# Unit 0's row maxima as own + relu(other - own) over three engines, and V's and Wo's products placed among the score products

## The reference

```python
def lora_linear(x, W, b, Bm, Am):
    out = jnp.einsum('bld,od->blo', x, W) + b
    upd = jnp.einsum('blr,or->blo', jnp.einsum('bld,rd->blr', x, Bm), Am)
    return out + SCALING * upd
x = _layernorm(x)                             # (1, 1024, 256)
q, k, v = (_split(lora_linear(x, W, b, B, A)) for q, k, v)   # 16 heads of 16
scores = jnp.einsum('bhqd,bhkd->bhqk', q, k) * SCALE
out = jnp.einsum('bhqk,bhkd->bhqd', jax.nn.softmax(scores, axis=-1), v)
x = x + lora_linear(out, Wo, bo, Bo, Ao)      # heads joined again
```

## Time and profile before

| | us |
|---|---|
| median of 3 runs | 350.2 (345.63 to 353.56) |
| profiled execution | 349.53 |
| its span, first to last instruction | 347.7 |
| busy: PE, DVE, ACT, POOL | 322.9, 280.4, 241.9, 128.5 |
| PE's mean granted clock | 0.97 of 2.4 GHz |

### The profile page before, as it was taken

The page is one execution under the profiler, slowest core; times in us unless marked ns, Lnnn a source line. Parts: engine busy times, 40 slices in busy tenths (PEclk is TensorE's granted clock), DMA queues, the critical chain, the costliest instruction groups (busy, mean ns, idle before and its releaser), DMA issues.

```text
span 347.7 us, 5546 instructions
## 1 busy us (share of the span) xinstructions
PE 322.9 (93%) x1919; PEld 141.8 (41%) x1919; DVE 280.4 (81%) x471; ACT 241.9 (70%) x465; POOL 128.5 (37%) x133
## 2 busy tenths in 40 slices
PE   7999789999999999999999899999998789699796
PEld 3753343222222222222222244359545645447695
DVE  6466998999999999999999345338689987988774
ACT  1576112888888898989888867994779323668694
POOL 5032018999300000000023001301699949994030
PEclk9999998999999999999999999999999969879899
DMA  7936855354132000000000000000000000000011
GB/s 216 326 51 129 144 166 86 63 117 84 21 78 45 3 0 3 0 3 0 0 3 1 3 1 2 0 2 0 1 2 0 1 0 2 0 2 0 1 62 60
DMA packets 14879, 14.57 MB, mean 42 GB/s; under 512 B 5060, under 2 KB 13191, under 8 KB 14663
## 3 DMA queue, kind: packets, MB, share of 16 engines
q1 hardware_dynamic: 12422, 12.09, 15.4%
q10 hardware_dynamic: 2176, 1.64, 1.6%
q0 software_dynamic: 256, 0.52, 0.9%
HBM read 5.78 MB, written 1.05 MB: 20 GB/s over the span
## 4 chain that ended last, share of the span: by engine, by line
PE 69%; DVE 14%; ACT 8%; POOL 5%; issue 3%; ACTq 0%; DVEq 0%; POOLq 0%
PE ps L1450 17%; PE ps L1436 13%; DVE mx L1126 9%; PE ps L1412 7%; PE ps L1582 6%; PE ps L1594 6%; PE ps L1363 4%; POOL pbuf L777 3%; PE ps L1567 3%; PE ps L1393 2%; PE ps L1626 2%; ACT ps L958 1%; PE ps L1352 1%; PE ps L1331 1%; ACT parts L898 1%
## 5 line engine op out<-in xcount | busy, mean ns | idle before, releaser
L1126 DVE TENSOR_REDUCE mx<-ps 128x1 f32<-128x1024 f32 x128 | 150.3, 1219 | 5.1 <-PE ps L1412 4.0
L913 ACT ACTIVATE pbuf<-ps 128x512 f32<-128x512 f32 x256 | 134.2, 604 | 24.6 <-PE ps L1436 23.6
L1436 PE MATMUL ps<-pack 64*128 64x512 f16 x256 | 75.9, 382 | 3.0 <-ACT pbuf L913 1.9
L1450 PE MATMUL ps<-pbuf,v_slot 128*32 128x512 f32 x512 | 68.0, 604 | 1.3 <-ACT parts L898 1.3
L1412 PE MATMUL ps<-pack 64*128 64x512 f16 x256 | 62.2, 388 | 4.5 <-DVE mx L1126 4.3
L1436 PEld LDWEIGHTS ps<-pack 64*128 64x128 f16 x256 | 18.8, 93 | 76.8 <-ACT pbuf L913 53.4
L777 POOL TENSOR_TENSOR pbuf<-wT 128x1024 f32<-128x1024 f32 (+3 forms) x32 | 48.2, 1533 | 4.7 <-ACT wT L987 4.7
L732 POOL COPY v_slot<-v_sb 128x512 f32<-128x512 f32 x8 | 4.8, 612 | 108.9 <-PE ps L1450 87.4
L708 POOL TENSOR_TENSOR rstd<-rstd,minus_half 128x2 f32<-128x2 f32 x16 | 11.4, 713 | 71.3 <-DVE rstd L1043 71.3
L1220 DVE SCALAR_TENSOR_TENSOR pack<-ps,g_unit,pack 128x512 f16<-128x512 f32 (+1 forms) x40 | 24.7, 640 | 14.5 <-ACT pack L970 14.5
L1582 PE MATMUL ps<-v_sb,w_nat 128*128 128x512 f16 (+1 forms) x160 | 32.7, 351 | 1.8 <-DVE v_sb L1212 1.8
(11 more groups left out here) (143 smaller groups left out, 370.4 us busy)
## 6 DMA issues: line engine op xcount, KB each, us to landing
w_nat<-in_L_ffn_w_dram SPq DMA_DIRECT2D x2, 1024.0 KB, 7.4
pack<-pbuf SPq DMA_DIRECT2D x24, 64.0 KB, 3.1
pack<-pack SPq DMA_DIRECT2D x3, 512.0 KB, 4.3
x_res<-in_L_attn_a_x_dram SPq DMA_DIRECT2D x4, 256.0 KB, 3.8
pack<-parts SPq DMA_DIRECT2D x16, 64.0 KB, 2.4
pack<-parts SPq DMA_DIRECT2D x32, 32.0 KB, 2.0
out_dram<-x_res SPq DMA_DIRECT2D x4, 256.0 KB, 2.1
w_nat<-in_L_attn_b_Wqkv_dram ACTq DMA_DIRECT2D x1, 768.0 KB, 6.3
```

Source lines behind the costliest of these rows:

```text
L913: act.activation(pbuf[:, c % 2, j, :], ps[:, b, :], ACT.Exp, scale=scale_reg).then_inc(drained[b], 1)
L1126: dve.tensor_reduce(mx[:, par, k:k + 1], ps[:, b:b + 2, :].rearrange("p b k -> p (b k)"), AX_X, ALU.max) \
L1436: pe.matmul(ps[:, b, :], k_group[rows, at, j, P * c:P * c + P].rearrange("p g t -> p (g t)"), q_rows[rows, at, qh, j, :].rearrange("p g t ...
L1450: ins = pe.matmul(ps[32 * j:32 * j + 32, PV_BANK, :], v_slot[:, qh, c, j, :], pbuf[:, c % 2, j, :], start=(c == 0), stop=(c == TT - 1))
```

## The change

Unit 0's maximum tiles are formed as own + relu(other - own), where "own" is the half of the keys that stands in the rows which the score matmul of that head reads. POOL multiplies the other rows of unit 0's queries by -1 (turn). PE's first matmul then goes over all 128 rows and gives own - other in the second bank; its second, over the own 64 rows, gives own in the first. ACT writes relu(other - own) to SBUF (take_over_own), and DVE adds that to own and takes the maximum in one instruction with an accumulator. All other units keep the plain maximum.

V is made in two parts: heads 0 to 3 for the eight token tiles in the maximum pass and the lead, heads 4 to 15 as entries of the score ring, one ahead of scores 4, 8, .. 24 of unit 0 and of 4 and 8 of unit 1. Wo's merge is such an entry too, ahead of score 12 of unit 1. V's own weight merge moves behind projections 4 and 5. ACT issues the first shift's transfer itself; later ones stay on SP, in other places of its queue. The Wqkv load goes to SP behind group 3. The thresholds are computed behind the lead's maxima. ACT's loop is unrolled, and ring places come from the planner instead of formulas. PE waits for a group's packing at the first maximum that reads it. Float16 terms and scratch space swap places in SBUF.

```diff
+V_PARTS = ((0, G), (G, H - G))
-KEEP_UP = 2
+KEEP_UP = 5
+BESIDE_FIRST_UNIT = [[] for _ in range(FILLS)]
+BESIDE_FIRST_UNIT[1] = [("proj", 6)]
+BESIDE_FIRST_UNIT[3] = [("proj", 7)]
+for _t, _k in enumerate(range(5, FILLS, 2)):
+    BESIDE_FIRST_UNIT[_k] = [("v", 0, _t)]
+BESIDE_LEAD = [[], [("shift", 0), ("wsum",)], [("v", 0, TT - 2)], [("v", 0, TT - 1)]]
+BESIDE_SCORES = {
+    **{(0, 4 * n + 4): ("v", 1, n) for n in range(TT - 2)},
+    (1, 4): ("v", 1, TT - 2), (1, 8): ("v", 1, TT - 1), (1, 12): ("wt", O_),
+}
...
+            def turn(rows, g, qh, first, last):
+                at = q_rows[rows, g, qh, :, :].rearrange("p j t -> p (j t)")[:, first:last]
+                pool.tensor_scalar(at, at, -1.0, 0.0, ALU.mult, ALU.add).then_inc(turned, 1)
...
+            for j in range(G):
+                pool.wait_ge(head_packed_by_pool[j], 32)
+                other = 1 - score_rows(j)
+                turn(slice(ROWS * other, ROWS * other + ROWS), 0, 0, HALF * j, HALF * j + HALF)
...
+            def take_over_own(u, k):
+                b = PAIR_BANKS[k % 2]
+                act.wait_ge(filled[b], base[b] + u * (FILLS // 2) + (k // 2 + 1))
+                act.activation(over_own[:, k % 2, :], ps[:, b + 1, :], ACT.Relu, scale=-1.0).then_inc(over_own_ready, 1)
...
+            for k in range(FILLS):
+                take_over_own(0, k)
+                if k == 3:
+                    evacuate_weight(V_)
+                for key in BESIDE_FIRST_UNIT[k]:
+                    beside(key)
...
+                if k == 1:
+                    land_shift(act, 0, 0, 0)
...
             def take_max(u, k, par):
                 b = PAIR_BANKS[k % 2]
+                if is_signed(u, k):
+                    dve.wait_ge(over_own_ready, FILLS * u + k + 1)
+                    slot = over_own[:, k % 2, :]
+                    dve.tensor_tensor_reduce(slot, ps[:, b, :], slot, scale=1.0, scalar=LOWEST, op0=ALU.add, op1=ALU.max,
+                                             accum_out=mx[:, par, k:k + 1]).then_inc(drained[b], 1)
+                    return
...
+                if is_signed(u, k):
+                    own = slice(ROWS * score_rows(j), ROWS * score_rows(j) + ROWS)
+                    pe.matmul(ps[:, b + 1, :], q_rows[:, g, qh, j, at], k_group[:, g, j, keys], start=True, stop=True)
+                    pe.matmul(ps[:, b, :], q_rows[own, g, qh, j, at], k_group[own, g, j, keys], start=True, stop=True) \
+                        .then_inc(filled[b], 1)
+                    return
```

More of the change, by code:

```diff
@@ L64 @@
 SHIFT_UNIT = 2.0 ** 15
+LOWEST = -3e38
+V_PARTS = ((0, G), (G, H - G))
 HALF_EXPONENT = 0x3F800000
@@ L112, in setup_order, with ring_keys, is_signed @@
     yield ("proj", 3)
-    yield ("wt", V_)
     yield ("proj", 4)
     yield ("proj", 5)
+    yield ("wt", V_)
 def beside_max_pass():
-    return [("proj", 6), ("proj", 7), *(("v", t) for t in range(TT)), ("wsum",), ("shift",), ("wt", O_)]
+    return [key for behind in (*BESIDE_FIRST_UNIT, *BESIDE_LEAD) for key in behind]
 SPLIT_BEHIND = {2: 6, 5: 7}
+BESIDE_FIRST_UNIT = [[] for _ in range(FILLS)]
[8 more added lines that the diff above has]
+}
+def ring_keys(u):
+    for s in range(STEPS):
+        if (u, s) in BESIDE_SCORES:
+            yield BESIDE_SCORES[u, s]
+        if s == SHIFT_AT and u < NU - 1:
+            yield ("shift", u + 1)
+        yield ("score", u, s)
+def is_signed(u, k):
+    return isinstance(u, int) and u == 0
 QUADS = H // 4
@@ L252, in numbered @@
     return of
-def ring_place(s, last):
-    return s + (s >= SHIFT_AT and not last)
-def ring_fills(place, i):
-    return (place - i) // len(SCORE_BANKS) + 1
 class Banks:
@@ L284, in plan_banks @@
         banks.count[b] += NU * FILLS // 2
-    for i, b in enumerate(SCORE_BANKS):
-        banks.count[b] += (NU - 1) * RING_USES + ring_fills(STEPS - 1, i)
+    ring = itertools.cycle(SCORE_BANKS)
+    for u in range(NU):
+        for key in ring_keys(u):
+            banks.claim(key, next(ring))
     banks.count[PV_BANK] += NU
@@ L566, in group_count, with land_shift @@
             return 16 * 3 * G * (1 if g < NG // 2 else TWO)
+        def land_shift(eng, g, qh, u):
+            is_drained(eng, ("shift", u))
+            n = G * TT // 2
+            for r in (0, 1):
+                rows = SHIFT_ROWS[g // 2]
+                rows = slice(ROWS * r + rows.start, ROWS * r + rows.stop, rows.step)
+                eng.dma_start(q_rows[rows, g, qh, 2 * r:2 * r + 2, :].rearrange("o h t -> o (h t)"),
+                              m_rows[n * r:n * r + n, :]).then_inc(shift_landed, 16)
         def part_is_cut(eng, m, c, s):
@@ L747, in _ @@
                     pool.wait_ge(tern_ready, 4 * n + c + 1)
+            for t in range(TT):
+                is_drained(pool, ("v", 1, t))
             for g in range(NG - 1):
@@ L1142, in _ @@
             cut_max(0, 0)
+            for k in range(LEAD):
+                take_max(1, k, 1)
             src = is_filled(dve, ("wsum",))
@@ L1365, in project @@
                 ins.then_inc(fill_sem(key), 1)
-            def add_bias(out, which):
-                at, n = BIAS_AT[which], 512 if which == "qk" else D
-                pe.matmul(out, onesb[0:NPART, 0:P], bias_rows[:, at:at + n], start=True, stop=False)
             def project_v(key):
-                t = key[1]
-                if t == 0:
+                _, part, t = key
+                first, n = V_PARTS[part]
+                cols = slice(HD * first, HD * first + HD * n)
+                if part == 0 and t == 0:
                     is_drained(pe, ("wt", V_))
@@ L1434, in score_tile @@
-                at = bass.ds(g, 1)
+                key = ("score", u, s)
                 rows = slice(ROWS * score_rows(j), ROWS * score_rows(j) + ROWS)
-                pe.matmul(ps[:, b, :], k_group[rows, at, j, P * c:P * c + P].rearrange("p g t -> p (g t)"),
-                          q_rows[rows, at, qh, j, :].rearrange("p g t -> p (g t)"), start=True, stop=True) \
-                    .then_inc(filled[b], 1)
+                pe.matmul(to_fill(pe, key), k_group[rows, g, j, P * c:P * c + P], q_rows[rows, g, qh, j, :], start=True,
+                          stop=True).then_inc(fill_sem(key), 1)
@@ L1452, in times_v, with beside @@
                 ins.then_inc(pv_chunk if c < TT - 1 else filled[PV_BANK], 1)
-            side = [key for key in beside_max_pass() if key[0] in ("proj", "v")]
+            def beside(key):
+                if key[0] == "shift":
+                    pe.wait_ge(consts, 6)
+                    shift_rows(key[1])
+                else:
+                    setup[key[0]](key)
             for k in range(FILLS):
@@ L1459, in _ @@
                     pe.wait_ge(head_packed_by_pool[k // 4], 32)
+                    pe.wait_ge(turned, k // 4 + 1)
                 max_tile(0, 0, 0, k)
-                if k % 3 != 2 and side:
-                    key = side.pop(0)
-                    setup[key[0]](key)
-            assert not side
+                for key in BESIDE_FIRST_UNIT[k]:
+                    beside(key)
             pe.wait_ge(second_half_packed, 16 * G)
```

204 lines of the change are left out of this document (83 added, 121 removed).

## The result

| | before | after |
|---|---|---|
| median, us | 351.3 (4 executions, 345.63 to 353.56) | 357.8 (4 executions, 357.33 to 358.33) |
| ratio | | 1.0285, 95% interval 1.0166 to 1.0404 |
| profiled execution | 349.53 | 357.33 |
| its span | 347.7 | 355.5 |
| busy: PE, DVE, ACT, POOL | 322.9, 280.4, 241.9, 128.5 | 330.3, 273.4, 253.2, 131.2 |

The changed kernel is slower by 2.9% (1.7 to 4.0); this ratio, like those of the experiments, leaves out executions more than 1.5% above the fastest of the same kernel, and the two medians alone lie 1.9% apart. The forecast was 1.5%, so the sign was right and the size too small; 357.8 lies just above the forecast's own range of 352 to 357.5. In the two traces the span grows by 7.8 us, where the sum had 5.2.

A forecast was written before the change was run, and what follows sets the result against it. DVE's maxima bound unit 0's pass and the units, where PE's slack is small too. 349.5 - 2.1 (A) - 1.2 (B) + 6.5 (C) + 2.0 (D) = 354.7 us; own range 352 to 357.5, with rivals 346.0 to 359.5.

The forecast's parts named there:

- the sum: Whole kernel: 349.5 - 2.1 - 1.2 + 6.5 + 2.0 = 354.7 us, 1.5% above the kernel before.
- A, the maximum pass: Unit 0's pass: maxima formed with relu replace 16 plain ones; the cut ends at 50.75 against 52.85, -2.1 us.
- The rings: Unit 0's pass: two tiles in flight through PE, ACT and DVE take 0.71 + 0.60 + 0.81 + 0.13 = 2.25 us.
- only exchanged with two projections: Unit 0's pass: despite the new place of V's merge, PE starts tile 0 at 29.25 as before.
- was almost free: V of heads 4 to 15 cost almost nothing where it lay before, since DVE was the slower engine there.
- B, the lead: Between unit 0's cut and the units: cut to end of tile 6 takes 8.5 instead of 9.7, -1.2 us.
- C, V among the scores: Units 0 and 1: eight V entries at 0.9 each, +7.2 us, less about 0.7 once: +6.5; bounds 0 and +11.
- the credit of 0.7 for a finished tile: Units: about 0.7 us saved once, as DVE finds a finished tile waiting when PE falls behind.
- D, Wo's merge: Unit 1: the merge as an entry costs 2.1 plus 0.1 less ACT's 0.2, +2.0 us; bounds 0 and 2.3.
- The units did not swallow the work: First rival: V and Wo's merge cost nothing in the units, under DVE's maxima; 346.2 us, chance 0.17.
- The paired instruction doesn't run at half rate: Second rival: in unit 0's pass DVE's paired sum and maximum takes 1.18 + 0.12 instead of 0.81; 357.8 us, chance 0.16.
- The third, PE's clock: Third rival: PE at its lower clock for 3 to 4 us around the lead costs up to 2; 356.7 us, chance 0.10.

The follow-up runs named there:

- e1: The changed kernel with unit 0's sixteen maxima plain again, without sign change or relu; V and Wo's merge stay in the units: 357.24 us.
- e2: The changed kernel with all of V beside the maximum pass again, Wo's merge in the lead, thresholds ahead of the lead's maxima: 351.61 us, ratio 1.0102.
- e10: The kernel before, with only the first shift's transfer issued by ACT behind its copy instead of by SP: 351.04 us, ratio 1.0012.
- e4: The changed kernel without the lead's five padding matmuls (KEEP_UP = 0): 353.02 us.
- e5: The changed kernel with three padding matmuls behind the cut's transposes instead of five ahead of the lead's first score: 355.01 us.
- e9: The changed kernel with three padding matmuls behind the cut's transposes instead of the lead's five, and V in two halves of eight heads: 351.55 us, ratio 1.0236.
- e6: The changed kernel with each entry, V's and Wo's, two scores later and the same work: 361.51 us.
- e12: e9 with Wo's merge back in the lead, behind the last V, and out of unit 1: 351.09 us, ratio 1.0145.
- e3: The changed kernel without V's two products in the eight entries for heads 4 to 15; bias product, ring place and copy stay: 350.64 us.
- e7: The changed kernel with V in two halves of eight heads, so entries have 128 columns instead of 192: 353.62 us.

## Why the prediction was right in sign and too small

**A, the maximum pass: better than the sum, and in the main for another reason.** The parts were close: 0.70 for DVE instead of 0.81, 0.60 for ACT. The rings came to 2.13 to 2.21 and not 2.25. What sets them is open: two signed tiles and V take PE 2.13 as worked out, and with 0.70 in place of 0.81 the sum's chain of three engines is 2.14. Eight tiles in four rings took 8.7 instead of 9.0; most of the 1.1 that A did better lies before, since tile 7 was finished at 40.4 and not 41.4, and wasn't taken apart. What the step named as the gain (DVE's cheaper maxima) is only about 1.1; 2.1 come without it (e1), 1.5 of them from the place of V's merge, which the step called "only exchanged with two projections". That V "was almost free" in the pass holds for the kernel before, where DVE's wait behind it is 0.28. Beside signed tiles it is not free: e2's cut starts 3.1 later than the changed kernel's.

**B, the lead: the step that failed first.** The step "from the cut to the end of tile 6 this is 8.5" forecast a gain of 1.2 and the lead lost 0.5. It failed in three ways. First, the base: 9.7 was taken as the work of the lead, and by e10 about 1.1 of it was the lower clock, for with the same work, and the transfer issued by ACT, it takes 8.56 at the full one. The sum knew the row at 0.50 and used it only as a bound. Second, the transfer: issued by ACT it is used 3.5 to 3.6 after its issue (e4, e5, e10). The 2.8 read from the earlier trace rows was right for SP's queue; why ACT's takes longer is not shown. Its earlier issue alone brings nothing that the times show (e10). Third, and this is what the miss comes from, the padding, put at nothing without a reason: KEEP_UP went from 2 per tile to 5 in one place, a line of the diff that the sum has no term for. Before, two stood behind each of five tiles; after, five stand together ahead of the first score, at the lower clock 2.34. Taken away from there, the lead is 8.8 (e4) or 8.6 (e5) long, and 8.3 at the full clock (e9), so all but 0.1 of B's miss is accounted for. Like for like, at the full clock, B is 8.56 (e10) to 8.34 (e9), a gain of 0.2.

**C, V among the scores: right in kind, too small by 1.6.** Three terms make that up, and with D they are as large as B's miss. Eight periods at 0.97 are 7.8 where the sum had 7.2 at 0.9; a wait for ACT, which was to vanish, is there again, though e6 doesn't show that it costs V's periods anything. The first of them lay at the lower clock and took 3.85, 0.5 more. And the credit of 0.7 for a finished tile is nearly missing (10.4 against 7.8 + 0.5 + 2.35 = 10.6). At the full clock it shows: from the lead's end to the end of unit 2's cut e9 takes 37.82 and e10 30.79, 7.0 apart, where 8 x 0.69 + 2.35 = 7.9.

**D, Wo's merge: 2.35 and not 2.0**, just above its upper bound of 2.3. Of the difference 0.14 goes with the place of the entry (e6). What leaving the lead gave back is 1.2 (e12).

**The rivals.** The units did not swallow the work: a period with V takes 3.36, far over 2.6, and e3 and e7 show its price to follow its columns. The paired instruction doesn't run at half rate. The third, PE's clock, was right in part: it was put at up to 2 around the lead and is 0.5 in the first V period of the profiled execution and, as an estimate, 1.1 in the padding (two such matmuls take 1.03 at the lower clock and 0.60 at the full one in the kernel before, five 2.34 here). Its chance, 0.10, was low for a kernel whose own runs differ by 8 us; the prediction read that spread in the table and never asked what made it.

**What stays open.** The low clock falls at other places in different executions of the same instructions: the program of e6 is that of the changed kernel up to unit 0, and was at 0.50 from 39.5 on, the changed kernel's from 52.9. Why is not shown, nor whether the changed kernel ever runs its lead at the full clock with its padding in place.
